# Row maxima of the first attention on two partition halves: shift and causal mask as 64-row products, with a negated half identity made per unit

## What is computed

```
q = rope(h @ Wq)   # 16 heads of 64
k, v = rope(h @ Wk), h @ Wv   # 4 heads of 64, each shared by 4 query heads
scores = where(causal, q @ k.T * 64**-0.5, -1e30)
out = softmax(scores) @ v @ Wo
```

## Time and profile before

| | us |
|---|---|
| median of 3 runs | 1860.3 |
| lowest and highest run | 1855.88, 1866.44 |
| span of the profiled execution | 1853.8 |
| median less span | 6.5 |
| PE, DVE, POOL, ACT busy in the span | 1628.6, 1054.7, 881.7, 703.7 |
| first attention | about 36 to 785 |

### The profile page before, as it was taken

The page is one execution under the profiler, slowest core; times in us unless marked ns, Lnnn a source line. Parts: engine busy times, 40 slices in busy tenths (PEclk is TensorE's granted clock), DMA queues, the critical chain, the costliest instruction groups (busy, mean ns, idle before and its releaser), DMA issues.

```text
span 1853.8 us, 75738 instructions
## 1 busy us (share of the span) xinstructions
PE 1628.6 (88%) x34444; PEld 1281.1 (69%) x34444; DVE 1054.7 (57%) x2235; ACT 703.7 (38%) x1135; POOL 881.7 (48%) x836
## 2 busy tenths in 40 slices
PE   6899999999999998888859878999989898978993
PEld 4567777777677766687747656777777677767883
DVE  3656666666687855537105446665666566544234
ACT  2333434434334333354423333433334333334331
POOL 2555555555555556446857652414233242016442
PEclk9999999999999999999979989999999999989997
DMA  9700000000000000052153524233241313026666
GB/s 305 255 14 2 8 2 8 2 8 2 8 2 8 2 6 19 14 145 39 45 103 45 100 38 91 60 67 78 49 93 42 83 48 87 16 83 187 208 205 185
DMA packets 103849, 128.05 MB, mean 69 GB/s; under 512 B 11909, under 2 KB 86281, under 8 KB 103064
## 3 DMA queue, kind: packets, MB, share of 16 engines
q1 hardware_dynamic: 82920, 103.39, 20.5%
q0 software_dynamic: 15808, 16.93, 4.8%
q10 hardware_dynamic: 4800, 2.89, 0.6%
HBM read 91.57 MB, written 54.07 MB: 79 GB/s over the span
## 4 chain that ended last, share of the span: by engine, by line
PE 59%; DVE 17%; DMA 7%; POOL 6%; issue 6%; ACT 4%; POOLq 0%; ACTq 0%; SPq 0%; DVEq 0%
PE psum L1170 55%; DVE colmax L1863 3%; DMA arena<-in_pack 3%; ACT prob L1616 2%; DMA added_rows<-arena,slot_token 2%; DVE colmax L1972 2%; DVE ctx_sum L1875 2%; DVE raw L1851 2%; DVE rowmax L1870 1%; POOL added_rows L2235 1%; DMA added_rows<-ffw,slot_token 1%; POOL arena L2223 1%; PE psum L1494 1%; POOL rope_a L2158 1%; POOL rope_b L2160 1%
## 5 line engine op out<-in xcount | busy, mean ns | idle before, releaser
L1170 PE MATMUL psum<-arena 128*32 128x32 f32 (+8 forms) x10296 | 568.9, 250 | 46.3 <-issue 25.1
L1170 PEld LDWEIGHTS psum<-arena 128*32 128x32 f32 (+3 forms) x10296 | 447.3, 125 | 132.9 <-issue 65.2
L1633 ACT ACTIVATE arena<-psum 128x1024 f32<-128x1024 f32 (+1 forms) x192 | 169.4, 882 | 319.0 <-PE psum L1170 317.0
L1972 DVE TENSOR_REDUCE colmax<-psum 128x256 bf16<-128x768 f32 (+2 forms) x160 | 178.3, 1114 | 83.0 <-PE psum L1170 80.4
L1170 PE MATMUL psum<-neg_ident,rowmax 128*32 128x128 bf16 (+3 forms) x4352 | 208.5, 248 | 7.1 <-issue 4.7
L1170 PE MATMUL psum<-prob,ffw 128*32 128x128 f32 x5120 | 201.5, 275 | 14.8 <-DVE rowmax L1870 13.3
L1863 DVE TENSOR_REDUCE colmax<-psum 128x512 bf16<-128x2048 f32 (+2 forms) x96 | 168.3, 1754 | 77.7 <-PE psum L1170 77.6
L1648 ACT COPY ctx_sum<-psum 128x384 f32<-128x384 f32 x128 | 61.3, 479 | 384.6 <-PE psum L1170 345.0
L2210 POOL TENSOR_TENSOR arena<-ctx_sum 128x256 f32<-128x256 f32 x128 | 94.4, 738 | 219.4 <-DVE ctx_sum L1875 207.8
L1980 DVE TENSOR_REDUCE rowmax<-psum 128x2 bf16<-128x256 f32 (+1 forms) x192 | 97.8, 510 | 139.8 <-PE psum L1170 139.8
L1616 ACT ACTIVATE prob<-psum 128x2048 f32<-128x2048 f32 (+3 forms) x128 | 158.5, 1239 | 26.3 <-PE psum L1170 25.8
(11 more groups left out here) (232 smaller groups left out, 2465.3 us busy)
## 6 DMA issues: line engine op xcount, KB each, us to landing
arena<-in_pack SPq DMA_DIRECT2D x39, 578.0 KB, 3.7
sent<-in_empty SPq DMA_DIRECT2D x9, 2112.0 KB, 41.3
arena<-qk_parts SPq DMA_DIRECT2D x96, 128.0 KB
q_copies<-arena SPq DMA_DIRECT2D x32, 256.0 KB
prob<-q_copies SPq DMA_DIRECT2D x128, 64.0 KB
qk_parts<-arena SPq DMA_DIRECT2D x16, 384.0 KB, 4.7
arena<-sent SPq DMA_DIRECT2D x39, 132.0 KB, 3.3
ffw<-in_L_w SPq DMA_DIRECT2D x16, 256.0 KB, 5.5
```

Of the source, the lines that this page charges most:

```text
L1170: return pe.matmul(o, lhsT, rhs, start=start, stop=stop, skip_group_check=True)
L1633: act.activation(probs_of(i)[:, :, h0 * P:(h0 + nh) * P], slot(n)[:, 0:(i + 1) * W].rearrange("p (j c) -> p j c", c=W), ACT.Exp, scale=HD1 ...
L1972: dve.tensor_reduce(colmax[:, n % 2, 0:W], slot(n)[:, 0:(i + 1) * W].rearrange("p (j c) -> p c j", c=W), AX.X, ALU.max).then_inc(colmax1_d ...
```

## The change

The row maxima are turned in a layout in which each partition half (`par`) holds the queries modulo 64 of that half's two heads, so that the shift can be made with 64-row products.

- maxima: 16 products of 32 weight columns instead of four of 128. Quarter `quad` of the partitions takes the 32 queries `low` of one half, of the heads of one `par`; the 128 columns x stand for head a and query half. DVE's reduction keeps its shape; its result is now [par and query mod 64, (a, half)].
- a new DVE operation, `spread`, multiplies `rowmax`, broadcast over 64 columns, with `neg_half` (minus one where the column is the partition modulo 64): 128x256 bf16. It waits on the new semaphore `rowmax_made`, and counts `max0_done` in place of the reduction.
- shift: for each pair of key blocks and each `par` one product of 64 rows of ones with `spread`, up to 512 columns. The two `par` go to different banks.
- causal mask: four 64-row products of 128 columns (`later_keys` with `neg_half`) instead of two 128-row products of 256.
- constants: the causal table is loaded in three 128x128 parts instead of one, with one more cast and one operation for `neg_half`.

```diff
-        "causal": np.where(p[:, None] <= p[None, :], 0.0, NEG).astype(np.float32),
+        "causal": np.stack([np.where(p[:, None] <= p[None, :], 0.0, NEG)] + [
+            np.where(p[:, None] % HQ + HQ * half >= p[None, :], 0.0, -NEG) for half in range(2)], 1).astype(np.float32),
...
-                        for par in range(2):
-                            ins = mm(scores_of(u)[:, par, i, :], ident_bf[:, :],
-                                     causal[:, :].unsqueeze(1).to_broadcast([P, 2, P]), False)
+                        for half in range(2):
+                            for par in range(2):
+                                rows = slice(HQ * par, HQ * (par + 1))
+                                ins = mm(scores_of(u)[:, par, i, :].rearrange("p (a q) -> p a q", a=2)[
+                                             :, :, HQ * half:HQ * (half + 1)],
+                                         later_keys[rows, half, :],
+                                         neg_half[rows, :].unsqueeze(1).to_broadcast([HQ, 2, HQ]), False)
                         ins.then_inc(scored, 1)
...
-                        for h in range(GRP):
-                            ins = mm(psum[:, CTX, h * P:(h + 1) * P], colmax[:, n % 2, h * P:(h + 1) * P],
-                                     ident_bf[:, :], start=(h == 0))
+                        for x in range(GRP):
+                            a, half = divmod(x, 2)
+                            for quad in range(GRP):
+                                par, low = divmod(quad, 2)
+                                at = (2 * par + a) * P + half * HQ + low * QUAD
+                                ins = mm(psum[QUAD * quad:QUAD * (quad + 1), CTX, x * P:(x + 1) * P],
+                                         colmax[:, n % 2, at:at + QUAD], ident_bf[:, :], start=(x == 0))
                         ins.then_inc(max0_full, 1)
...
-                        for h in range(GRP):
-                            par, a = divmod(h, 2)
-                            for j in range(0, i + 1, 2):
-                                nj = min(2, i + 1 - j)
-                                ins = mm(scores_of(u)[:, par, j:j + nj, a * P:(a + 1) * P],
-                                         rowmax[:, n % 2, h:h + 1].to_broadcast([P, P]),
-                                         neg_ident[:, :].unsqueeze(1).to_broadcast([P, nj, P]), False)
+                        for j in range(0, i + 1, 2):
+                            nj = min(2, i + 1 - j)
+                            for par in range(2):
+                                rows = slice(HQ * par, HQ * (par + 1))
+                                ins = mm(scores_of(u)[:, par, j:j + nj, :].rearrange("p j (x q) -> p j x q", q=HQ),
+                                         ones_bf[rows, :],
+                                         spread[rows, n % 2, :, :].unsqueeze(1).to_broadcast([HQ, nj, GRP, HQ]), False)
                         ins.then_inc(shifted, 1)
...
                         dve.tensor_reduce(rowmax[:, n % 2, :], psum[:, CTX, :].rearrange("p (h k) -> p h k", h=GRP),
-                                          AX.X, ALU.max).then_inc(max0_done, 1)
+                                          AX.X, ALU.max).then_inc(rowmax_made, 1)
+                        w.wait_ge(rowmax_made, n + 1)
+                        dve.tensor_tensor(
+                            spread[:, n % 2, :, :], rowmax[:, n % 2, :].unsqueeze(2).to_broadcast([P, GRP, HQ]),
+                            neg_half.unsqueeze(1).to_broadcast([P, GRP, HQ]), ALU.mult).then_inc(max0_done, 1)
```

More of the change, by code:

```diff
@@ L31 @@
 GRP = 4
+HQ = P // 2
 E, F = 8, 512
@@ L232, in build @@
         prob = sb("prob", [P, 2, 4 * BANK])
-        causal_f = prob[:, 0, 0:P]
+        causal_f = prob[:, 0, 0:3 * P].rearrange("p (a c) -> p a c", a=3)
         colmax = sb("colmax", [P, 2, BANK], BF16)
@@ L337, in build @@
         xn1 = ctx_sum[:, 1, 1, :].rearrange("p (n d) -> p n d", n=NT)
+        spread = ctx_sum[:, 1, 0, :].bitcast(BF16)[:, 0:2 * GRP * HQ].rearrange("p (z h q) -> p z h q", z=2, h=GRP)
+        neg_half = ctx_sum[:, 1, 1, 0:HQ // 2].bitcast(BF16)
+        later_keys = ctx_sum[:, 1, 1, HQ // 2:HQ // 2 + P].bitcast(BF16).rearrange("p (a c) -> p a c", a=2)
         small = raw[:, 1, :]
@@ L1005, in build @@
             semaphore(n) for n in ("x_full", "x_loaded", "moments_ready", "normed", "rot_a", "swapped", "key_rest"))
+        rowmax_made = semaphore("rowmax_made")
         scored, colmax_dve, colmax_act, max0_full, max0_done, shifted, prob_ready, ctx_full, ctx_drained, recip = (
@@ L1785, in _ @@
                         dve.tensor_scalar(neg_ident[:, :], ident[:, :], -1.0, None, ALU.mult)
+                        dve.scalar_tensor_tensor(neg_half, ident[:, 0:HQ], -1.0, ident[:, HQ:P], ALU.mult, ALU.subtract)
                     elif k == "mod_first":
@@ L1813, in _ @@
                         w.wait_ge(d_x, XREST)
-                        dve.tensor_copy(causal[:, :], causal_f).then_inc(consts_ready, 1)
+                        dve.tensor_copy(causal[:, :], causal_f[:, 0, :])
+                        dve.tensor_copy(later_keys, causal_f[:, 1:3, :]).then_inc(consts_ready, 1)
                     elif k == "stat":
```

## The result

| | before | after |
|---|---|---|
| median, us | 1859.3 (4 runs) | 1901.56 (4 runs) |
| lowest and highest | 1855.88, 1866.44 | 1895.85, 1911.41 |
| span of the profiled execution | 1853.8 | 1894.0 |
| first attention, from the first Exp's start to the last's end | 746.65 | 784.72 |
| behind it, to the end of the span | 1065.5 | 1068.7 |

The changed kernel is slower: ratio 1.0229, interval 1.0193 to 1.0265. The forecast was 1874 with 1849 to 1895; slower was right, and the time lies 6.6 us above the range. Nearly all of the loss is in the first attention: 38.1 of the 40.2 us between the profiled executions. The code behind it is the same in all kernels of this study, and its stretch took from 1062 to 1078 us in their profiles, so the length of the first attention, and of each step in it, is read beside the medians.

The account below looks back on a forecast made before the run. PE, busy 97%, was not yet taken as the bound: each kind of step had its own limit among PE, Exp and DVE. Terms summed to +1.49 a batch, +11.9 in eight, plus 2 for selection: 1874 us median, range 1849 to 1895.

Parts of the forecast that it names:

- the operation's 0.42: Added two-input DVE operation of 128x256 behind the reduction: 0.42 us, 0.455 with its wait; between 0.19 and 0.69.
- its turns with POOL: DVE and POOL exclude each other on two-input SBUF operations; a blocked new operation ends about 0.28 behind POOL's.
- the shift in overlapping pairs: Shift products on two 64-row groups run together: -0.43 in four-block steps, -0.32, -0.21, -0.11 for three, two, one.
- the mask at -0.21: Causal products as two 64-row pairs, -0.11, with no change of rows ahead of them, -0.10: -0.21 a unit.
- the values' wait: Values wait for the new DVE operation, 0.4 to 0.8 in two-block steps; their total wait well above 21 us.
- Four-block steps: Four steps of a batch, forecast at -0.48, +0.47, -0.32 and +0.01: together -0.32.
- two-block steps: Values stand 0.05 + 0.455 behind the reduction, POOL sometimes in the way: 0.39, 0.39, 0.38, 0.71, together +1.87 a batch.
- three-block steps: Shift -0.32 and causal products -0.21 make -0.53 a step, four times, -2.12 a batch.
- one-block: the DVE chain gets 0.455 longer ... POOL is free there: One-block steps, bound by DVE alone: 0.455 each, plus 0.12 in two of four, +2.06 a batch.
- I estimate 2 us: Two batches with expert selection on DVE: more steps become DVE-bound, about four steps of 0.5, 2 us.

Follow-up runs that it names:

- TensorE's part alone: The changed kernel without the new DVE operation; the shift adds products of a constant zero tile: 1848.77 us, ratio 0.9934.
- the mask alone: The kernel before with only the causal products as four 64-row products, maxima, shift and reduction unchanged: 1853.43 us, ratio 0.9959.
- the operation behind the signal: The kernel before plus the added VectorE operation after max0_done is counted, result unused: 1902.4 us; with two POOL rotation products cut to 16 columns, 1881.94.
- the waits filled: The changed kernel with dummy bf16 products ahead of the maxima in sixteenth steps and five one-block steps of the selection batches: 1894.48 us, ratio 1.0186.

## Why the prediction was right and wrong

Right were the operation's 0.42 and its turns with POOL, the shift in overlapping pairs, the mask at -0.21 in the four- and three-block steps, and the values' wait. The sum over fifteen of sixteen steps came out too, about +1 forecast and +0.75 to +1.0 measured, but by luck, for by kinds of step the errors cancel. Four-block steps lost 0.6 together where they were to gain 0.32; two-block steps lost 0.7, not 1.87; three-block steps gained 0.15 to 0.22 each, not 0.53; and the one-block steps 4, 8 and 12 lost 0.2 together, not 0.455 each. With TensorE's part alone the three-block steps gain 0.22, as with the mask alone: the shorter shift shows in none of them.

The step that failed is in two terms.

- "one-block: the DVE chain gets 0.455 longer ... POOL is free there". That was read at the first one-block step and used for all four. In the sixteenth the layer norm follows on the queue, and was done as POOL began its rotation. Pushed by 0.45, it takes 3.57 instead of 1.88. Six such steps cost 15.0 where the term has about 3. Cutting POOL's two products brings the step to 7.4, and with the operation behind the signal from 12.0 to 7.3, while the kernel before keeps its length: shown, not argued. Some 1 us of the 15.0 is the clock's, which falls in three of the six steps (9.84 and 10.02 come back to 9.44 and 9.42 with the waits filled, 10.23 only to 10.18). Moving the layer norm gave back 5.7 us of attention, and moving the projection lost 12 and 20: each other place has a waiter too.
- "I estimate 2 us" for the batches with the selection. They lost 16.9 beside their sixteenth steps, and 16.7 of it stands in nine of these 46 steps: the fourth, eighth and twelfth of the sixth batch, the fourth, eighth, tenth and fourteenth of the seventh, and the fourth and eighth of the eighth. Six of the nine hold a fall of the clock, which the prediction didn't have at all. Four of these six are seen without it too, with the same code around them. The eighth and twelfth of the sixth take 7.35 and 7.85 with the layer norm moved, instead of 8.18 and 9.52; the tenth and fourteenth of the seventh take 8.10 and 7.43 with the waits filled, instead of 9.77 and 9.10. That is 5.8 us of the clock's, and in the last two steps it is nearly the whole loss (7.85 and 7.48 before the change). How the other 11 us divide between VectorE's fuller queue and the two falls in the eighth batch stays open, and so does the cause of the 2.8 us of the first batch.

The prediction asked, for the wait, who stands behind the new operation and named column maximum, shuffle and reciprocal. The layer norm, there once a batch, was missing from that list.

## What to carry to other kernels

An operation put on a queue costs what it makes late, and the dearest can be a rare step: list what follows it in every iteration of the period, not in a typical one, and look at what the other engine starts just after. Where two engines take turns, a delay of 0.45 cost 2.7 here. Look at the granted clock before a longer step is put down to a wait: the same products took 9.5 us instead of 6.3 behind one. And before bundling three edits, price each alone: here the mask carried most of the gain and needed none of the cost.

## What the runs showed of the hardware

- Four-operation layer norm beside POOL products of two SBUF inputs: 0.33 each when free, 1.30 and 1.42 when a POOL product of 1.3 us was running or started; the two engines go one by one. A reduction with one input took 0.555 to 0.558 throughout. By the Trainium skill (SBUF — State Buffer, "Who interferes with whom") a `tensor_scalar` can take the port pair that VectorE shares with GpSimd, and a `tensor_reduce` on this chip never does; the runs agree with both, with the numbers above.
- TensorE's granted clock fell from 2.4 to 1.2 GHz for 3.4 us, at times 6.8 or more, at or just behind waits in which it was idle for 1.5 to 2.2 us, in eight of the nine cases of the changed kernel; the ninth, in the twelfth step of the sixth batch, follows two waits of 0.73 and 0.90. In the six sixteenth steps of the second to seventh batch it is idle for 1.54 us each time; the clock falls in the second, fourth and seventh and not in the other three. In the seventh batch of the kernel before, products 1.8 and 2.1 us apart were followed by no fall; in the version with the mask alone, products 1.9 us apart were. The length of one wait doesn't decide it.
- Two bf16 products of 64 rows and 512 columns on two row halves and two banks start 3 ns apart, the next pair 0.227 us behind.
